# Rounding the split operand earlier, taking its remainder last, and one image done whole instead of in halves

## The reference

```
cA, cH, cV, cD = dwt2(x)                      # one Haar level: four bands of 16 x 16
proc = lambda c: batchnorm_relu(einsum('bchw,oc->bohw', c, conv_w), ...)
rimg0 = idwt2(proc(cA), proc(cH), proc(cV), proc(cD))      # "r"
rimg1 = x put together again from its own wavelet bands    # equals x
y = conv3x3(concatenate([rimg0, rimg1], axis=1), convW_w) + convW_b
y = batchnorm_relu(y, ...)                    # statistics over all 16 images
z = median of the 3 x 3 neighbourhood of y (zero padded)
out = y + einsum('bchw,oc->bohw', z, W) + b
```

## Time and profile before

| | |
|---|---|
| median of 3 runs | 418.56 us (416.46 to 419.51) |
| profiled execution, its own time | 416.29 us |
| its span, first to last instruction | 414.0 us |
| mean granted PE clock | 0.992 |
| PE busy | 392.0 us, 95% |
| DVE busy | 371.7 us, 90% |
| POOL busy | 217.1 us, 52% |
| ACT busy | 168.0 us, 41% |
| chain that ended last: PE / POOL / DVE | 75% / 9% / 6% |

### The profile page before, as it was taken

How to read it: one execution, slowest core, us unless ns; L and a number is a source line. 1 busy time by engine, 2 the same in 40 slices (tenths; PEclk the granted TensorE clock), 3 DMA queues, 4 the chain that set the end, 5 groups by cost and what they waited for, 6 DMA issues and landing times.

```text
span 414.0 us, 3845 instructions
## 1 busy us (share of the span) xinstructions
PE 392.0 (95%) x1202; PEld 224.7 (54%) x1202; DVE 371.7 (90%) x528; ACT 168.0 (41%) x364; POOL 217.1 (52%) x208
## 2 busy tenths in 40 slices
PE   7889977999999998999999999999999999996994
PEld 2335556886744444464645555555646598852441
DVE  3899850899987999999999999999999999989897
ACT  2565852242424443341514333334323322363871
POOL 3999389062553437485755747575743440032251
PEclk9999996999999999999999999999999999999999
DMA  7980100010010010101011010101010000003555
GB/s 299 409 331 3 51 0 1 2 51 0 2 51 21 30 51 2 51 0 51 2 51 51 1 52 1 51 0 51 2 51 20 30 2 1 2 0 146 212 225 228
DMA packets 7794, 26.70 MB, mean 65 GB/s; under 512 B 992, under 2 KB 1248, under 8 KB 7776
## 3 DMA queue, kind: packets, MB, share of 16 engines
q1 hardware_dynamic: 7776, 26.48, 16.8%
HBM read 18.09 MB, written 8.39 MB: 64 GB/s over the span
## 4 chain that ended last, share of the span: by engine, by line
PE 75%; POOL 9%; DVE 6%; issue 4%; ACT 3%; DMA 2%; SPq 0%; POOLq 0%; DVEq 0%
PE conv_ps L426 59%; PE conv_ps L447 9%; PE conv_ps L535 3%; PE one_ps L408 2%; POOL y L245 2%; POOL y L246 2%; DMA z<-x 2%; PE conv_ps L538 1%; ACT z L605 1%; DVE y L992 1%; POOL ru L346 1%; POOL eo L340 1%; POOL y L385 1%; POOL eo L339 1%; POOL ru L345 1%
## 5 line engine op out<-in xcount | busy, mean ns | idle before, releaser
L426 PE MATMUL conv_ps<-ru,wt 128*128 128x512 f32 (+1 forms) x360 | 132.4, 504 | 0.0
L426 PEld LDWEIGHTS conv_ps<-ru,wt 128*128 128x128 f32 x360 | 69.0, 192 | 49.8 <-issue 45.7
L426 PE MATMUL conv_ps<-xu,wt 128*128 128x496 f32 (+3 forms) x240 | 89.1, 508 | 5.3 <-POOL taps_lo L361 5.3
L642 ACT ACTIVATE y<-conv_ps,sgn 128x512 f32<-128x512 f32 (+1 forms) x40 | 25.5, 637 | 153.6 <-PE conv_ps L426 153.6
L426 PEld LDWEIGHTS conv_ps<-xu,wt 128*128 128x128 f32 x240 | 46.5, 195 | 41.5 <-issue 33.2
L351 POOL TENSOR_TENSOR x_lo<-y,x_hi 128x1024 fp32r<-128x1024 f32 x10 | 23.7, 2366 | 50.5 <-DVE one_ps L901 41.1
L426 PE MATMUL conv_ps<-ru,v 128*128 128x496 f32 (+3 forms) x120 | 43.8, 500 | 1.5 <-POOL ru L253 1.5
L345 POOL TENSOR_TENSOR ru<-eo 128x512 f32<-128x512 f32 x16 | 17.0, 1062 | 53.2 <-DVE one_ps L859 53.1
L535 PE MATMUL conv_ps<-z,w 128*128 128x512 f32 x64 | 29.7, 596 | 5.7 <-DVE y L992 3.4
L408 PE MATMUL one_ps<-y,w 128*128 128x512 f32 x64 | 30.4, 605 | 4.9 <-DVE z L739 2.6
L605 ACT ACTIVATE z<-z,bn 128x256 f32<-128x256 f32 x64 | 33.0, 591 | 0.4 <-DVE bn L804 0.4
(11 more groups left out here) (141 smaller groups left out, 745.5 us busy)
## 6 DMA issues: line engine op xcount, KB each, us to landing
z<-x SPq DMA_DIRECT2D x16, 512.0 KB, 10.7
raw_place<-x SPq DMA_DIRECT2D x15, 512.0 KB, 3.3
out<-y SPq DMA_DIRECT2D x15, 512.0 KB, 2.6
wt<-w_t SPq DMA_DIRECT2D x2, 576.0 KB, 10.6
ru<-x SPq DMA_DIRECT2D x1, 512.0 KB, 14.0
out<-y SPq DMA_DIRECT2D x2, 256.0 KB, 2.1
w<-w_t SPq DMA_DIRECT2D x2, 64.0 KB, 8.0
vec<-vectors SPq DMA_DIRECT2D x1, 3.0 KB, 9.3
```

Of the source, the lines that this page charges most:

```text
L426: return nc.tensor.matmul(bank(u, b)[:, (r0 - row) * BW:(r1 - row) * BW], taps(half, kx, ky), plane[:, (r0 + dy) * BW:(r1 + dy) * BW], sta ...
L642: S.activation(at(slot(n), row * W + b, [[2, cols]]), src, ACT.Identity, scale=sgn[:, :], accum_out=y_sum[:, part:part + 1]).then_inc(y_ke ...
```

## The change

1. **ACT** rounds x of image 2 (`round_x(2)`) right after the statistics of stage 1, ahead of the square root, and no longer after the normalisation of image 2.
2. **POOL** makes `x_lo` of image 2 and both halves of `taps_lo` ahead of `ru03` of images 0 and 1, and no longer behind them.
3. **PE** no longer waits for `taps_lo` ahead of the first `outputs`. It waits for it inside `pq` of image 2.
4. **PE**, in every split image, takes the products with `x_hi` first, then those with r, then those with `x_lo`. POOL makes `ru12` before `x_lo` for images from 6 on. The buffer `x_hi` is given free by `q_done` of the split image before.
5. Image 14 joins `SPLIT` and leaves `HALVED`: it is one unit of 32 rows. There are 19 units instead of 20.
6. Both halves of image 15 get their seeds inside the median of image 13, the first in its middle, the second near its end.

```diff
-    SPLIT = (2, 3) + tuple(range(6, 14))
+    SPLIT = (2, 3) + tuple(range(6, 15))
-    HALVED = (0, 1, IMAGES - 2, IMAGES - 1)
+    HALVED = (0, 1, IMAGES - 1)
...
             for n in range(2):
                 make_xu03(n)
+            make_lo(2)
+            for b in range(2):
+                pool.wait_ge(hi_taps_made, b + 1)
+                G.tensor_tensor(tap_part(taps_lo, b), whole_taps(b), tap_part(fl(taps_hi), b), ALU.subtract).then_inc(lo_taps_made, 1)
             pool.wait_ge(x_edges_made, 2)
             for n in range(2):
                 make_ru03(n)
-            for b in range(2):
-                pool.wait_ge(hi_taps_made, b + 1)
-                G.tensor_tensor(tap_part(taps_lo, b), whole_taps(b), tap_part(fl(taps_hi), b), ALU.subtract).then_inc(lo_taps_made, 1)
-            make_lo(2)
 
             for n in range(2, IMAGES):
                 if n > 3:
                     pool.wait_ge(mids_read, last_unit(n - 3) + 1)
-                    if n in SPLIT:
-                        make_lo(n)
...
                 make_ru12(G, n).then_inc(ru12_made, 1)
-                if n == 3:
+                if n in SPLIT[1:]:
                     make_lo(n)
...
+            def split_pq(u, b, done):
 
                 n = UNITS[u][0]
                 pe.wait_ge(x_hi_made, SPLIT.index(n) + 1)
...
+                split_products(u, b, x_hi, taps_hi, start=True)
+                if n == SPLIT[0]:
+                    pe.wait_ge(lo_taps_made, b + 1)
+                split_products(u, b, x_hi, taps_lo)
+                if b == 0:
+                    pe.wait_ge(ru12_made, n + 1)
+                for ky in KY_ORDER:
+                    product(u, b, R_HALF, (None, 1)[b], planes(ru12[n % 2][:, :])[b], ky)
+                pe.wait_ge(x_lo_made, SPLIT.index(n) + 1)
+                split_products(u, b, x_lo, taps_hi, stop=True).then_inc(done, 1)
...
-            pe.wait_ge(lo_taps_made, 2)
             for u in range(2, len(UNITS) + 1):
...
+            def round_x(n):
+
+                if n != SPLIT[0]:
+                    act.wait_ge(q_done, last_unit(SPLIT[SPLIT.index(n) - 1]) + 1)
+                S.activation(x_hi[:, :], slot(n), ACT.Identity).then_inc(x_hi_made, 1)
+
+            wait_xu12(act, SPLIT[0])
+            round_x(SPLIT[0])
             act.wait_ge(var1_ready, 1)
...
             last = len(UNITS) - 1
-            del EARLY[last - 3], EARLY[last - 2]
-            LATE[last - 4], EARLY[last - 3] = last - 1, last
+
+            del EARLY[last - 2]
+            LATE[last - 3] = last
```

More of the change, by code:

```diff
@@ L434, in pq_of_x, with split_products @@
                 product(u, b, X_HALF, (None, 1)[b], plane, ky, start=ky == KY_ORDER[0])
-            def split_pq_of_x(u, b):
+            def split_products(u, b, part, parts_taps, start=False, stop=False):
+                for ky in KY_ORDER:
+                    dy = ky - 1
+                    r0, r1 = max(0, -dy), min(H, H - dy)
+                    col = (b * KY + ky) * CH
+                    mm = nc.tensor.matmul(bank(u, b)[:, r0 * BW:r1 * BW], parts_taps[:, col:col + CH],
+                                          part[:, b * HALF + (r0 + dy) * BW:b * HALF + (r1 + dy) * BW],
+                                          start=start and ky == KY_ORDER[0], stop=stop and ky == KY_ORDER[-1])
+                return mm
+            def split_pq(u, b, done):
                 n = UNITS[u][0]
                 pe.wait_ge(x_hi_made, SPLIT.index(n) + 1)
-                for part, parts_taps in ((x_hi, taps_hi), (x_hi, taps_lo), (x_lo, taps_hi)):
-                    if part is x_lo:
-                        pe.wait_ge(x_lo_made, SPLIT.index(n) + 1)
-                    for ky in KY_ORDER:
-                        dy = ky - 1
-                        r0, r1 = max(0, -dy), min(H, H - dy)
-                        col = (b * KY + ky) * CH
-                        mm = nc.tensor.matmul(bank(u, b)[:, r0 * BW:r1 * BW], parts_taps[:, col:col + CH],
-                                              part[:, b * HALF + (r0 + dy) * BW:b * HALF + (r1 + dy) * BW],
-                                              start=parts_taps is taps_hi and part is x_hi and ky == KY_ORDER[0], stop=False)
-                if b == 1:
-                    mm.then_inc(x_parts_read, 1)
+                split_products(u, b, x_hi, taps_hi, start=True)
[4 more added lines that the diff above has]
+                    pe.wait_ge(ru12_made, n + 1)
+                for ky in KY_ORDER:
+                    product(u, b, R_HALF, (None, 1)[b], planes(ru12[n % 2][:, :])[b], ky)
+                pe.wait_ge(x_lo_made, SPLIT.index(n) + 1)
+                split_products(u, b, x_lo, taps_hi, stop=True).then_inc(done, 1)
             def pq_of_r(u, b, done):
@@ L463, in pq @@
                     pe.wait_ge(squares_summed, 2 * (u - 2) + b + 1)
+                    if UNITS[u][0] in SPLIT:
+                        split_pq(u, b, done)
+                        continue
                     if UNITS[u][0] in PRE:
                         pe.wait_ge(pre_put, 2 * PRE.index(UNITS[u][0]) + b + 1)
-                    elif UNITS[u][0] in SPLIT:
-                        split_pq_of_x(u, b)
                     else:
@@ L665, in put_early @@
                              ACT.Identity).then_inc(pre_put, 1)
-            def round_x(n):
-                place = SPLIT.index(n)
-                act.wait_ge(x_parts_read, place)
-                S.activation(x_hi[:, :], slot(n), ACT.Identity).then_inc(x_hi_made, 1)
-            round_x(2)
             for u in range(len(UNITS)):
```

1 line of the change is left out of this document (removed).

## The result

The changed kernel takes 411.93 us (median of four runs, 411.49 to 414.02); the kernel before, run beside it, took 417.90 us (416.46 to 419.51). The ratio is 0.9873, with a 95% interval of 0.9831 to 0.9915: 1.3% faster. Predicted were 414.0 us and -4.6 us; the ratio says -5.3 us (-3.6 to -7.1), the two medians -6.0.

The account below looks back on a forecast made before the run. PE was taken to set the pace in most of stage 2, alternating with ACT and DVE in stage 3. Terms -7.8 - 1.9 - 1.2 + 6.3 = -4.6 us gave 414.0 us against the median; range 410 to 418.5 us.

Parts of the forecast that it names:

- The start: Start of stage 2: PE's 5.3 us idle and 2.85 us of low clock go, less 0.3 us delay; gain 7.8 us.
- The delay of `bn1_ready`: First normalisation: DVE's small instructions wait for POOL's, making `bn1_ready` up to 3.2 us late, mostly covered on PE.
- the start gains half: Rival at stage 2's start: longer DVE waiting leaves PE a gap and low clock; gain 3.3 us, 418.5 us total; chance 0.15.
- Image 6: `pq` of image 6: `ru12` made first lets the r products begin sooner; gain 1.9 us (1.0 to 2.2).
- Image 14 on PE: Stage 2: image 14 whole and split takes PE 9.08 us instead of two `pq` of 5.07; gain 1.1 to 1.2 us.
- Stage 3: Price of image 14 whole behind the second normalisation: 6.3 us given back (4.2 to 9.1).
- the longer rest: Stage 3: 32 rows, not 18, remain before the first `finish`, which comes 4.2 us later and passes fully to the end.
- the low clock: Stage 3: PE's wait grows to about 7.3 us and the clock falls behind it; cost 1.1 us (0 to 2.9).
- POOL's blocking: Stage 3: POOL's `map_x1` now stands beside two median instructions with both inputs in SBUF; cost 1.0 us (0 to 2).
- The wait at the moved seeds: DVE near the end of image 13's median: waits about 4 us for PE's `pq`, free since the second normalisation stays on time.
- Stage 3 absorbs the longer rest: Rival: second `finish` and `mix` move less, clock doesn't fall, price only 1 to 2 us; about 409 us; chance 0.12.
- Slow clock in stage 3: Rival: 0.50 granted through most of 28 us of products; beyond 9 us the gain is gone, 423 us at 20; chance 0.08.

Follow-up runs that it names:

- Run 1: Kernel before with parts 1 to 3 alone, the new start of stage 2: 411.14 us, 0.9845 against before.
- run 3: Changed kernel with its start taken back (remainders, rounding and PE's wait where they were): 419.57 us, 1.0043 against before.
- run 4: Changed kernel with POOL making `ru03` of image 0 ahead of the remainders, out of the way of the chain to `bn1_ready`: 411.93 us, 0.9856 against before.
- Run 6: Changed kernel without part 4, `x_lo` ahead of r again on PE and POOL: 413.67 us, 0.9922 against before.
- run 7: Changed kernel with each `finish` placed four steps earlier, the first at 12: 413.71 us, 0.9919 against before.
- run 8: Changed kernel with the first three additions at 12, 15 and 18 and the other six at 23 to 38: 410.24 us, 0.9800 against before.
- run 9: Changed kernel with the last seeds behind the second instruction of image 14's median and the second normalisation at 10, not 7: 409.45 us, 0.9784 against before.
- run 10: Run 9 with the first three additions at 14, 15 and 16 and the rest spread from 24 to 41: 405.09 us, 0.9696 against before.
- run 5: Changed kernel with 50 instead of 30 products on zeros ahead of PE's first `mix`: 411.88 us, 0.9870 against before.
- run 2: Changed kernel without part 5 and its seeds (parts 5 and 6 taken back), image 14 in halves: 409.07 us, 0.9779 against before.

## Why the prediction was right, by its own steps

**The start, -7.8 predicted, 7.79 us measured.** Both halves came: the idle stretch and the low clock behind it. Run 1 shows the term alone (6.5 us in the time; 7.79 in the trace, of which 1.7 went again in image 6), run 3 takes it away (+7.6 in the time, 6.7 in the trace). So the start is worth 6 to 8 us, and how much of the low clock it saves differs between executions. The delay of `bn1_ready` that I worked out from one DVE row (up to 3.2 us) was 2.83 us, on three instructions of the five. The rule quoted there, Trainium skill, page SBUF — State Buffer, section Who interferes with whom, agrees with the measurement, down to instructions of one element a partition (1.40 us for 0.15). The rival that the start gains half is out: PE lost 0.3 us to the delay in after, and run 4, which removed it, started `pq` of image 2 only 0.5 us sooner.

**Image 6, -1.9 predicted, 1.54 measured.** r came 0.50 us after the `x_hi` products. Not predicted was the pitch, +0.05 us per split image, +0.35 in all. I had written that images 7 to 13 wouldn't change. Run 6 shows this is part 4's doing: with the old order the pitch is 19.17 us. The row above shows where it may come from (behind r the three products on `x_lo` take 1.15 us, the three on `taps_lo` behind `x_hi` 0.84), but no run takes the two apart. Part 4 is worth 1.7 us in the times and 1.2 us in the traces (run 6).

**Image 14 on PE, -1.2 predicted.** What is left of PE's 7.55 us is 7.55 - 5.20 - 1.54 + 0.35 = 1.16 us. It is a remainder; no run has this part without the seeds of part 6.

**Stage 3, +6.3 predicted, 5.66 measured.** By terms: the longer rest 4.30 us (predicted 4.2), the low clock 1.4 us (1.1). The 4.30 are 11.19 - 6.32 less the 0.57 below. For the clock I take the time from the second `finish` to the `mix` behind the first addition that PE makes itself: 4.55 us (374.05 to 378.60) for 3.13 in before (377.42 to 380.55), and DVE's idle time in the fourth `finish` grew by the same 1.4 us. It is a reading of two traces and not a test. POOL's blocking was predicted at 1.0 us and was -0.1: one instruction of the rest took 0.57 us more (L905, 1.34 us), and 0.67 us went at the place that was blocked before (there 1.06 us for 0.39). PE's wait is 6.48 us (7.3).

**The sum.** -7.79 - 1.54 + 0.35 - 1.16 + 5.66 = -4.5 us, with -4.6 predicted. None of the four terms is off by more than 0.7 us; inside the last one POOL's blocking is off by 1.1. That the total agrees within 0.1 us is luck: up to the end of stage 2 PE gained 10.1 us with stage 1 taken out, 0.8 less than predicted, and stage 3 gave back 0.6 less.

**The step that was wrong** is the reason given for the price: that the later first `finish` passes to the end in full because PE waits for it. I read PE's wait of 1.61 us as the limit of stage 3. In run 7 PE's two waits at the front are 1.29 and 2.73 us instead of 6.48, it goes on 5.2 us sooner, and the last `mix` starts when it did (50.9 us behind stage 2, 51.0 in after). PE's wait at the front and DVE's work up to the last median both end at the last `mix`, and the second was the longer: in every trace the last `mix` starts 1.6 us behind the end of the last median. I had dismissed DVE's idle time in stage 3, "since PE causes it"; that idle time was a term of the price, 1.4 us of it (4.5 us against 3.15): run 8 cut it with the blocking, and runs 9 and 10 cut it and the rest ahead of the first `finish`. The size came out right, as I read it, because both paths had grown by about the same in after: both contain the rest of image 14's median. For this reason the right number doesn't speak for the reason that I gave. The wait at the moved seeds, which I called free, was free only in that DVE was still in time for the normalisation. With its 3.76 us used for the median and the normalisation later by three instructions, the last `mix` comes 3.6 us forward (run 9).

**The rivals.** Stage 3 absorbs the longer rest: no, 5.66 us is near my forecast; but a different placing absorbs it entirely. Slow clock in stage 3: it came, at 0.50 to 0.68 from 370 to 379 us, which is about 7 us at the low level, some 5.6 of them with PE at work (from 372.29 us). It cost about 1.4 us. The rival needed over 9 us at the low level. 1.00 was back from 379 us on. The Trainium skill, page TensorE: Matmul & The Clock Gate, section What's actually happening, agrees in that: low after idleness, full again once PE works.

**What stays open.** What the low clock costs by itself in stage 3: run 5 shortened it and didn't prevent it. Why the last `mix` meets the low clock in some kernels and not in others (last section). Whether image 14 in halves would gain from new places for its additions as the whole image did wasn't tried, so part 5's worth at its best is known only as run 10 against run 2, 0.9696 against 0.9779.

## What to carry to other kernels

A wait of the busiest engine isn't yet the limit: before calling a term its price, ask which chain the *last* wait ends with, and how much work that chain's engine still has. Where an engine works in order, time that it waits at one place is free only if nothing behind it is late; here 3.76 us of waiting at a pair of seeds and 4.5 us in additions were worth 6.8 us of 411.9 once seeds, normalisation and additions were re-placed. When an edit changes the size of a piece of work, numbers that place other work by counting instructions (`FINISH_AT`, `BN3_AT`) should be set anew. With them left alone, image 14 whole gained 1.2 us on PE and cost about 3 us in all (run 2); with them and the seeds' place changed, the kernel took 405.09 us.
